# Clamps that subtract the decay first, exponentials without a bias, and a new order of a recurrent block's steps

## What is computed

```
xn = layernorm(x)
k_in = xn*mix_k + shifted*(1-mix_k)      # v_in, r_in likewise; shifted = xn one position earlier
k, v, r = k_in @ Wk, v_in @ Wv, sigmoid(r_in @ Wr)
td = -exp(time_decay)
step:  max_out = max(mx, k + tf)
       out = (exp(mx-max_out)*num + exp(k+tf-max_out)*v) / (exp(mx-max_out)*den + exp(k+tf-max_out))
       max_st = max(mx + td, k)
       e1s, e2s = exp(mx + td - max_st), exp(k - max_st)
       num, den, mx = e1s*num + e2s*v, e1s*den + e2s, max_st
s = (r * out) @ Wo
h = relu(xn @ w1 + b1);  z = h @ w2 + b2
g = silu(layernorm(xn + z) * gamma + beta)
result = x + s * g
```

## Time and profile before

| | |
|---|---|
| median of 3 runs | 125.14 us (123.63 to 125.21) |
| profiled execution | 125.17 us |
| its span, first to last instruction | 123.3 us |
| mean granted TensorE clock | 0.97 of full speed |

### The profile page before, as it was taken

The page is one execution under the profiler, slowest core; times in us unless marked ns, Lnnn a source line. Parts: engine busy times, 40 slices in busy tenths (PEclk is TensorE's granted clock), DMA queues, the critical chain, the costliest instruction groups (busy, mean ns, idle before and its releaser), DMA issues.

```text
span 123.3 us, 1619 instructions
## 1 busy us (share of the span) xinstructions
PE 105.7 (86%) x336; PEld 57.8 (47%) x336; DVE 98.1 (80%) x199; ACT 97.3 (79%) x157; POOL 84.9 (69%) x104
## 2 busy tenths in 40 slices
PE   5998999599954899998999994499998999899570
PEld 5982554434621455554545470254643464535240
DVE  1659893998992984986998988094997999988992
ACT  2367775999497946996999971999699779999970
POOL 2039999999999997797299999409799373015000
PEclk9999999999999689999999999779999999999999
DMA  3999000000000000002000000000002020050034
GB/s 97 265 308 253 14 3 0 0 5 3 0 3 0 0 0 0 0 0 85 0 0 0 8 0 0 0 0 0 3 0 85 0 73 14 0 170 0 5 110 145
DMA packets 9449, 5.09 MB, mean 41 GB/s; under 512 B 480, under 2 KB 9184, under 8 KB 9440
## 3 DMA queue, kind: packets, MB, share of 16 engines
q1 hardware_dynamic: 8880, 4.59, 13.1%
q10 hardware_dynamic: 560, 0.40, 1.4%
HBM read 2.89 MB, written 2.10 MB: 40 GB/s over the span
## 4 chain that ended last, share of the span: by engine, by line
POOL 41%; issue 24%; ACT 15%; PE 14%; DVE 2%; POOLq 1%; ACTq 0%; DVEq 0%
POOL xn L338 10%; POOL gap_max L392 10%; POOL gap_min L385 6%; POOL step_x L368 4%; PE bank L558 4%; POOL xT_lo L359 3%; ACT hid L471 3%; POOL xT_hi L352 2%; POOL dv L399 2%; ACT L424 2%; POOL keep L407 2%; PE bank L626 2%; PE bank L609 1%; PE bank L589 1%; ACT g L544 1%
## 5 line engine op out<-in xcount | busy, mean ns | idle before, releaser
L640 PE MATMUL bank<-hid,w_c 128*128 128x512 f32 x64 | 32.0, 608 | 0.1
L589 PE MATMUL bank<-mixed,w_in 128*128 128x512 f32 x48 | 24.1, 598 | 0.4 <-POOL mixed L377 0.4
L471 ACT ACTIVATE hid<-bank,vec 128x512 f32<-128x512 f32 x32 | 20.9, 680 | 3.4 <-PE bank L611 2.6
L609 PE MATMUL bank<-xT_hi,w_hi 128*128 128x512 f32 x28 | 17.8, 635 | 4.6 <-ACT hid L471 2.3
L720 DVE SCALAR_TENSOR_TENSOR mixed<-step_x,vec,bank 128x511 f32<-128x511 f32 x24 | 17.4, 732 | 0.5 <-POOL step_x L368 0.5
L640 PEld LDWEIGHTS bank<-hid,w_c 128*128 128x128 f32 x64 | 12.1, 196 | 11.6 <-issue 10.7
L744 DVE TENSOR_TENSOR_SCAN den<-e_keep,e_new 128x512 f32<-128x512 f32 x8 | 10.4, 1304 | 7.8 <-ACT e_new L500 5.4
L338 POOL TENSOR_SCALAR xn<-x_sb,neg_mean,rstd 128x128 f32<-128x128 f32 x28 | 15.4, 561 | 0.1
L392 POOL TENSOR_SCALAR gap_max<-gap,td 128x512 f32<-128x512 f32 x8 | 14.9, 1867 | 0.0
L385 POOL TENSOR_SCALAR gap_min<-gap,td 128x512 f32<-128x512 f32 x8 | 13.1, 1638 | 2.6 <-DVE gap L737 2.6
L626 PE MATMUL bank<-sq,averager 128*128 128x512 f32 (+1 forms) x18 | 9.4, 608 | 4.8 <-ACT hid L471 4.8
(11 more groups left out here) (70 smaller groups left out, 211.3 us busy)
## 6 DMA issues: line engine op xcount, KB each, us to landing
x_sb<-x SPq DMA_DIRECT2D x7, 256.0 KB, 5.9
block_out<-res SPq DMA_DIRECT2D x7, 256.0 KB, 2.3
w_in<-squares SPq DMA_DIRECT2D x1, 256.0 KB, 3.1
w_in<-w ACTq DMA_DIRECT2D x1, 256.0 KB, 5.2
w_in<-w SPq DMA_DIRECT2D x1, 256.0 KB, 6.1
block_out<-res SPq DMA_DIRECT2D x2, 128.0 KB, 1.9
x_sb<-x ACTq DMA_DIRECT2D x1, 128.0 KB, 2.9
x_sb<-x SPq DMA_DIRECT2D x1, 128.0 KB, 2.7
```

The source lines that it names most:

```text
L471: act.activation(hid[b % 2][:, f, :], ps(f"up{f}", b)[:, :], ACT.Relu, bias=vec[:, B1_COLUMN + f:B1_COLUMN + f + 1]).then_inc(done[f"hid{f ...
L589: pe.matmul(ps(name, b)[:, :], w_in[:, which, :], mixed[b % 2][:, which, :], start=True, stop=True).then_inc(done[name], 1)
L609: pe.matmul(dst, hi, xT_hi[n][:, :], start=True, stop=False)
L640: ins = pe.matmul(ps("z", b)[:, :], w2_c[:, f, :], hid[b % 2][:, f, :], start=False, stop=last, skip_group_check=True)
```

## The change

Both clamps get a second operation: first td is subtracted from gap, then the minimum (or maximum) with zero is taken. The exponentials then need no bias: e_new = Exp(gap_min), e_keep = Exp(-gap_max). Each of the four down-projection chunks signals its own end (z0 to z3) where only the last one did, and hid of block b waits for its own chunk of block b-2. The orders of all engines and the table of banks are new; the table loads on ACT are 6 of each set now, since th_r of block 0 stands with the other tanhs. Every other step is there as often as before. A constant FP32_MAX is added and not used.

```
-                pool.tensor_scalar(gap_min[n][:, :], gap[n][:, :], td[:, :], None, ALU.min).then_inc(done["gmin"], 1)
+                pool.tensor_scalar(gap_min[n][:, :], gap[n][:, :], td[:, :], 0.0,
+                                   ALU.subtract, ALU.min).then_inc(done["gmin"], 1)
...
-                pool.tensor_scalar(gap_max[n][:, :], gap[n][:, :], td[:, :], None, ALU.max).then_inc(done["gmax"], 1)
+                pool.tensor_scalar(gap_max[n][:, :], gap[n][:, :], td[:, :], 0.0,
+                                   ALU.subtract, ALU.max).then_inc(done["gmax"], 1)
...
-                    after(act, "z", b - 2)
+                    after(act, f"z{f}", b - 2)
...
-                act.activation(e_new[n][:, :], gap_min[n][:, :], ACT.Exp, bias=neg_td[:, :]).then_inc(done["e_new"], 1)
+                act.activation(e_new[n][:, :], gap_min[n][:, :], ACT.Exp).then_inc(done["e_new"], 1)
...
-                act.activation(e_keep[n][:, :], gap_max[n][:, :], ACT.Exp, bias=td[:, :],
-                               scale=-1.0).then_inc(done["e_keep"], 1)
+                act.activation(e_keep[n][:, :], gap_max[n][:, :], ACT.Exp, scale=-1.0).then_inc(done["e_keep"], 1)
...
     "act": """
-        ln_exp ve:0 rs:0 xT:0 neg_td w1_hi wo ve:1 rs:1 hid2:0 hid1:0 hid3:0 hid0:0 xT:1 silu_set th_r:0
-        ln_exp ve:2 v_sb:0 rs:2 e_keep:0 e_new:0 hid1:1 hid2:1 hid0:1 ln_den:0 sq:0 hid3:1 xT:2 silu_set
-        th_g:0 th_a:0 ln_exp ln_var:0 xT:3 rstd2:0 ve:4 hid3:2 e_new:1 sq:1 hid0:2 e_keep:1 hid1:2 rs:4
+        ln_exp ve:0 neg_td rs:0 xT:0 w1_hi wo ve:1 rs:1 hid0:0 hid2:0 hid1:0 xT:1 hid3:0 v_sb:0 ve:2
+        rs:2 hid3:1 e_new:0 e_keep:0 hid2:1 hid0:1 hid1:1 ln_den:0 silu_set th_g:0 th_r:0 sq:0 xT:2
+        th_a:0 ln_exp ln_var:0 e_new:1 rstd2:0 sq:1 ve:4 xT:3 hid1:2 rs:4 hid2:2 ln_var:1 e_keep:1
...
     "dve": """
-        bnA:0 bnB:0 aggr1:0 norm1:0 bn:1 aggr1:1 ink:0 cols w2_sum inr:0 bn:2 bn:3 inv:0 mx:0 aggr1:2
-        gap:0 aggr1:3 inv:1 bn:4 bn:5 ink:1 den:0 aggr1:4 aggr1:5 bn:6 inr:1 rel:0 aggr1:6 mx:1 ink:2
+        bnA:0 bnB:0 aggr1:0 norm1:0 bn:1 aggr1:1 inr:0 ink:0 w2_sum inv:0 bn:2 bn:3 cols aggr1:2 mx:0
+        aggr1:3 gap:0 ink:1 bn:4 inr:1 den:0 bn:5 aggr1:4 rel:0 bn:6 inv:1 mx:1 aggr1:5 gap:1 dev:0
+        aggr1:6 bn:7 adev:0 aggr1:7 wkv:0 inv:2 ink:2 zn:0 gated:0 inr:2 den:1 mx:2 rel:1 ink:3 zn:1
+        inv:3 dev:1 adev:1 gap:2 wkv:1 mx:3 gap:3 prod:0 gated:1 inr:3 ink:4 res:0 den:2 inv:4 den:3
...
     "pool": """
-        d:0 w1_lo nm:1 norm1:1 fix:0 w2_c xT_hi:1 d:1 fix:1 xT_lo:1 nm:2 gmax:0 gmin:0 norm1:2 norm1:3
-        d:2 dv:0 fix:2 keep:0 xT_hi:2 xT_lo:2 gmax:1 gmin:1 gmin:2 xT_hi:3 d:3 gmax:2 xT_lo:3 nm:4 dv:1
+        d:0 w1_lo nm:1 norm1:1 fix:0 w2_c xT_hi:1 xT_lo:1 d:1 gmin:0 gmax:0 fix:1 nm:2 norm1:2 norm1:3
+        dv:0 keep:0 xT_hi:2 gmin:1 xT_lo:2 d:2 gmax:1 d:3 nm:4 xT_hi:3 fix:2 xT_lo:3 dv:1 norm1:4 keep:1
+        fix:3 norm1:5 gmax:2 gmin:2 d:4 xT_hi:4 xT_lo:4 gmin:3 gmax:3 fix:4 dv:2 norm1:6 d:5 keep:2
...
```

More of the change, by code:

```diff
@@ L42 @@
[L42 to L46, removed]
@@ new lines @@
+        th_r:1 sq:2 hid2:3 ln_exp e_keep:2 ln_var:2 e_new:2 hid1:3 e_new:3 e_keep:3 rstd2:2 hid3:4
+        v_sb:2 xT:5 ln_den:2 hid1:4 ln_den:3 silu_set th_g:2 hid2:4 v_sb:3 th_a:2 th_r:2 silu:2 hid0:4
+        th_r:3 th_g:3 sq:3 th_a:3 ln_exp e_new:4 ln_var:3 e_keep:4 rstd2:3 hid2:5 xT:6 sq:4 v_sb:4
+        e_keep:5 e_new:5 hid0:5 hid3:5 ln_var:4 xT:7 ln_den:4 rstd2:4 ln_den:5 hid1:5 silu_set th_g:4
+        th_r:4 silu:3 hid1:6 th_a:4 hid3:6 hid2:6 silu:4 th_g:5 v_sb:5 hid0:6 sq:5 th_r:5 th_a:5 ln_exp
@@ L52 @@
[L52 to L56, removed]
@@ new lines @@
+        inv:3 dev:1 adev:1 gap:2 wkv:1 mx:3 gap:3 prod:0 gated:1 inr:3 ink:4 res:0 den:2 inv:4 den:3
+        zn:2 prod:1 rel:2 mx:4 inr:4 gap:4 rel:3 dev:2 ink:5 adev:2 wkv:2 mx:5 dev:3 gated:2 adev:3
+        gap:5 wkv:3 inv:5 zn:3 gated:3 prod:2 den:4 ink:6 inr:5 den:5 rel:4 zn:4 mx:6 gap:6 inv:6 ink:7
+        dev:4 adev:4 rel:5 wkv:4 gated:4 inr:6 mx:7 gap:7 inv:7 dev:5 res:1 adev:5 wkv:5 inr:7 res:2
+        den:6 gated:5 den:7 zn:5 zn:6 prod:3 rel:6 rel:7 prod:4 res:3 dev:6 adev:6 res:4 wkv:6 gated:6
@@ L59 @@
+        dev:7 adev:7 prod:5 prod:6 wkv:7 res:5 zn.a:7 gated:7 zn.b:7 res:6 prod.a:7 prod.b:7 res.a:7
+        res.b:7
     """,
     "pool": """
-        d:0 w1_lo nm:1 norm1:1 fix:0 w2_c xT_hi:1 d:1 fix:1 xT_lo:1 nm:2 gmax:0 gmin:0 norm1:2 norm1:3
-        d:2 dv:0 fix:2 keep:0 xT_hi:2 xT_lo:2 gmax:1 gmin:1 gmin:2 xT_hi:3 d:3 gmax:2 xT_lo:3 nm:4 dv:1
-        norm1:4 keep:1 fix:3 norm1:5 xT_hi:4 xT_lo:4 d:4 keep:2 gmin:3 gmax:3 dv:2 fix:4 d:5 norm1:6
-        xT_hi:5 fix:5 keep:3 dv:3 xT_lo:5 gmax:4 gmin:4 d:6 xT_hi:6 gmin:5 gmax:5 xT_lo:6 fix:6 norm1:7
@@ L65 @@
-        dv:4 keep:4 gmin:6 d:7 dv:5 gmax:6 fix:7 xT_hi:7 keep:5 xT_lo:7 gmin:7 gmax:7 dv:6 keep:6 dv:7
+        d:0 w1_lo nm:1 norm1:1 fix:0 w2_c xT_hi:1 xT_lo:1 d:1 gmin:0 gmax:0 fix:1 nm:2 norm1:2 norm1:3
+        dv:0 keep:0 xT_hi:2 gmin:1 xT_lo:2 d:2 gmax:1 d:3 nm:4 xT_hi:3 fix:2 xT_lo:3 dv:1 norm1:4 keep:1
+        fix:3 norm1:5 gmax:2 gmin:2 d:4 xT_hi:4 xT_lo:4 gmin:3 gmax:3 fix:4 dv:2 norm1:6 d:5 keep:2
+        gmax:4 gmin:4 fix:5 dv:3 keep:3 xT_hi:5 xT_lo:5 norm1:7 gmin:5 gmax:5 d:6 xT_hi:6 xT_lo:6 fix:6
@@ L66 @@
+        dv:4 xT_hi:7 d:7 keep:4 gmin:6 fix:7 xT_lo:7 dv:5 keep:5 gmax:6 gmin:7 gmax:7 dv:6 keep:6 dv:7
         keep:7
@@ L216, in build_block @@
                  + [f"up{f}" for f in range(NF)] + [f"hid{f}" for f in range(NF)]
-                 + ["z", "sq", "var", "ln_var", "rstd2", "zn", "silu", "prod", "back", "res"])
+                 + [f"z{f}" for f in range(NF)] + ["sq", "var", "ln_var", "rstd2", "zn", "silu", "prod", "back", "res"])
         done = {n: sem(f"done_{n}") for n in STEPS}
@@ L247, in bank_free, with chunks_of @@
                     after(eng, step, previous[2], previous[1])
+        def chunks_of(b):
+            return [name for name, _, i in tokens("pe") if name in CHUNKS and i == b]
         def cut(half):
@@ L477, in square @@
                 once(act, b, "cols", 4)
-                after(act, "z", b)
+                after(act, chunks_of(b)[-1], b)
                 after(act, "var", b - 2)
@@ L631, in step @@
                     once(pe, b, "w2", 1)
-                    order = [name for name, _, i in tokens("pe") if name in CHUNKS and i == b]
-                    if order[0] == f"z{f}":
+                    if chunks_of(b)[0] == f"z{f}":
                         for step in ("xT", "ink", "inv", "inr"):
@@ L638, in step @@
                     after(pe, f"hid{f}", b)
[L639 to L643, removed]
+                    pe.matmul(ps("z", b)[:, :], w2_c[:, f, :], hid[b % 2][:, f, :], start=False,
+                              stop=chunks_of(b)[-1] == f"z{f}", skip_group_check=True).then_inc(done[f"z{f}"], 1)
                 return step
```

42 lines of the change are left out of this document (21 added, 21 removed).

## The result

The changed kernel takes 130.22 us (median of 4 runs, 128.76 to 130.86) against 124.51 us: a ratio of 1.038, 95% interval 1.023 to 1.054. It is slower by 3.8%. The forecast was 117.2 us with a range of 113.8 to 127.0; the time lies outside it, where the second rival stood (129.0, range 127 to 131.5).

A forecast was written before the change was run, and what follows sets the result against it. Bound by GpSimd first, a mixed middle, then DVE with ACT. 125.17 - 7.6 (DVE's waits behind exponentials) - 0.4 (exponentials without bias) = 117.2 us, the new order counted as zero; range 113.8 to 127.0.

The forecast's parts named there:

- the second rival: GpSimd gets slower: the second operation is its own pass, clamps take 1,950 ns; 129.0 us, range 127 to 131.5; chance 0.17.
- What bounds the kernel: Whole span: GpSimd limits first (12 to 47 and 68 to 80 us), then a mixed middle, DVE with ACT last.
- The clamp: GpSimd's gap_min and gap_max: subtract then min or max takes 690 ns instead of 1,560; chance six in ten.
- The upper bound: Highest cost considered for the new GpSimd clamp: the present clamp plus one more pass at keep's rate, 1,950 ns.
- What the cheaper clamp is worth: In GpSimd's two full stretches, DVE's waits behind the exponentials go: -7.6 us.
- the ceiling: DVE's idle time in GpSimd's two full stretches, 5.8 and 3.6 us, 9.4 in all, as the most a cheaper clamp gains.
- POOL's chain of 11.4 us: Shortening of GpSimd's chain by ten clamps at 690 ns in its two full stretches, 18.3 to 6.9 us.
- The exponentials: On ACT, 719 to 625 ns each without bias column, 1.5 us less ACT; half of 0.9 us counted, -0.4 us.
- The new order: Changed orders on all engines, two table loads fewer on ACT (2.6 us), other banks: counted as zero, at best -0.5 us.
- the first rival: The clamp costs what it did, the order gives perhaps 1 us: 124.2 us, range 122 to 127; chance 0.23.
- The walk of block 0: Block 0 followed in the new order: gap_min starts near 16.7 us, gap_max ends near 18.1, den starts near 18.8.
- The third: Clamps are cheap, but PE's new queue holds back k and DVE waits for that: 121.4 us; included in the forecast's 0.60.

The follow-up runs named there:

- cheap stand-in: Both clamps as mult by 0, add 0, exponentials all one: in the kernel before 110.31 us, ratio 0.887; in the changed kernel 111.46 us, ratio 0.894.
- min-max clamps: Clamps as minimum then maximum, one of them with the largest float: in the kernel before 112.58 us, ratio 0.905; in the new order 113.93 us, ratio 0.912.

## Why the prediction was wrong, step by step

**What bounds the kernel.** Right. GpSimd first, in the two stretches named; from each row of the table to the next the clamp moves the time, in either order.

**The clamp** is the step that failed. It read: "I take 690 ns. By form (two stages, a column and an immediate) keep and xn are the nearest rows." The form was the wrong measure of nearness. Keep is mult-add and xn is add-mult, both among four ordered pairs that are fast; none of the pairs with a subtraction is. Of the two causes that the step offered for the present clamp the second is right: a single stage is dear, for each of the four operations tried (1,489 to 1,573 ns). But the step took from it that a filled second stage is cheap, and outside the four pairs it is dearer still. The upper bound, one more pass on top of the present clamp, gave 1,950 ns; it measured 2,000, just beyond it. The 690 ns are real, but for a clamp that the change doesn't use (679 to 690 for min-max).

**What the cheaper clamp is worth.** Wrong too, hidden behind the first: 7.6 us counted, 9.4 named as the ceiling. The cheap stand-in in the old order gave 125.06 - 110.31 = 14.8 us, for 16 x 0.94 = 15.0 us of clamps and 1.5 of ACT. The min-max clamps, which cost the 690 ns that the step reckoned with, gave 125.50 - 112.58 = 12.9 us. In the forecast's own order and without the bias such a clamp would be at 113.93 - 0.6 = 113.3 us, an estimate from the two runs above: below even the low end of 113.8. The 7.6 us of den's waits did go (7.7). What failed is that nothing else was counted: the ceiling was DVE's idle time in two stretches only, and the sentence that a clamp doesn't touch the wait for k was wrong, as the 2.8 us of mx and 2.4 us of prod show. POOL's chain of 11.4 us was nearer, and still low: it had ten clamps of the sixteen.

**The exponentials.** Right: 623 and 628 ns, 1.5 us of ACT, and 0.6 us in the time where 0.4 was counted; measured with GpSimd off the path.

**The new order.** Counted as nothing. With the old clamps it gives 0.9 us, near the "perhaps 1" of the first rival; with the dear ones 3.5, with the stand-ins it costs 1.2. The table loads are 12 and ACT's 94.0 us near the forecast; what the two loads taken out are worth by themselves no run shows. The walk of block 0 had gap_min start at 16.7 us; it was 17.16 in the changed kernel and 16.7 with the min-max clamps in this order. Its den, forecast for 18.8, started at 21.97 in the changed kernel, later than the 21.34 of before.

**The rivals.** The first (the clamp costs what it did) is nearly the run of the order alone, which keeps the bias as well: 124.2 forecast, 123.99 measured. But its condition wasn't met. The second (a second pass per operation) is what happened, 129.0 forecast, 130.22 measured. That its price was nearly right is luck, two errors that cancel. The clamps alone cost 8.8 us in the old order, not 4.3, which is 1.25 us of time per us of clamp instead of 0.68 (1.0 by the profiled executions, 131.97 - 125.17 = 6.8 us for 6.9 us of clamps). And the order gave 3.5 back. The share of a group in the chain is thus no bound on what its growth costs. Its counter-evidence, xn with two operations at 1.1 ns per column, was the misread row. The third (the gain stays in PE's queue) falls: mx waits 0.5 us for k with the stand-in in either order, 0.8 and 1.6 us with the min-max clamps.

The Trainium skill's rule of the port's rate for bodies of at most two operations (GPSIMD Engine Reference, section 3.1) holds here for the four pairs only (617 to 767 ns) and not for single operations (1,489 and up) or the other pairs (1,914 and up). For add-mult with two columns the traces give (767 - 447) / 384 = 0.83 ns per column between 128 and 512 columns. Nor does the time simply grow with the operations, as the forecast read the rule's second half: it does from 1,489 to 1,930 ns, but a multiplication alone takes 1,489 and a multiplication with an addition 626.

**What stays open.** Why these four pairs and not others is not shown by any run; the rows show only which. The list covers the pairs tried, on 128x512 tiles of float32. Why a clamp's growth costs its own time or more in the old order wasn't taken apart. The granted clock is lower there (0.95 to 0.96 against 0.97 to 0.99), which may be a part of it, as the higher clock with cheap clamps (0.98 to 1.00) may be of their gain; no run separates it. Nor does a run tell the effect of the order from that of the banks and semaphores that came with it.

## What to carry to other kernels

Take an instruction's cost on GpSimd from a row with the same ordered pair of operations; a row of the same shape and operand kinds can be off by a factor of three. Before an operation is folded into another on this engine, time the pair alone, and look whether a neutral second stage (a maximum with the lowest float, an addition of zero) makes a dear single stage cheap. Where one engine feeds the queues of all others, its lateness returns in waits that carry other engines' names, so a ceiling from one engine's idle time in a few stretches is too low.

## What the runs showed of the hardware

On GpSimd a filled second stage can take less than half the time of an empty one: minimum with a column alone 1,568 ns, the same minimum followed by a maximum 682. Order matters: min-max with two columns 762 ns, max-min 2,070. VectorE does the clamp without and with the subtraction in 486 and 480 ns, so there the second operation costs nothing:

```profile
L93 DVE TENSOR_SCALAR dve_min_col<-x_sb,vec 128x512 f32<-128x512 f32 x3 | 1.5, 486 | 80.7 <-POOL sub_min L84 80.6
L94 DVE TENSOR_SCALAR dve_sub_min<-x_sb,vec 128x512 f32<-128x512 f32 x3 | 1.4, 480 | 0.0
```

And clamps meet VectorE's instructions. All three stretched clamps of the changed kernel (2.90 us at 28.69, 2.90 at 53.93, 3.36 at 68.28) began while VectorE ran dev, den or rel, whose two inputs are both tiles in SBUF, and ended 1.7 to 1.8 us after the scan among them had ended. At 68.28 rel was running, and this scan came right behind it:

```profile
68.28 3.36 POOL L399 TENSOR_SCALAR gap_max<-gap,td 128x512 f32<-128x512 f32 x1 [2.02 <-DVE gap L741]
```

```profile
68.70 1.22 DVE L763 TENSOR_TENSOR_SCAN dev<-keep,dv 128x512 f32<-128x512 f32 x1
```

Four clamps that were 0.37 us or more under way when a scan of den or dev began (82.44, 92.69, 99.55 and 103.51 us) took 2.00 or 2.01 us. So what counts in these rows is which of the two has started first. The scans stretch too. This one ran beside xT_lo until 53.95 us and beside a clamp behind it, and took 1.68 us where the next den took 1.23; which of the two slowed it the rows don't tell:

```profile
53.35 1.68 DVE L748 TENSOR_TENSOR_SCAN den<-e_keep,e_new 128x512 f32<-128x512 f32 x1
```
